# Causal attention: the order of VectorE's work inside one turn

## The reference, cut to what matters

```
k = (x @ Wk).reshape(B, H, T, hs)
q = (x @ Wq).reshape(B, H, T, hs)
v = (x @ Wv).reshape(B, H, T, hs)
wei = jnp.einsum('bhtd,bhsd->bhts', q, k) * scale
mask = jnp.tril(jnp.ones((T, T), dtype=bool))
wei = jnp.where(mask, wei, -jnp.inf)
wei = jax.nn.softmax(wei, axis=-1)
out = jnp.einsum('bhts,bhsd->bhtd', wei, v).reshape(B, T, C)
return out @ Wp + bp                        # added to the tokens
```

## Time and profile before

| | |
|---|---|
| median of 3 runs | 1110.09 us (1109.1 to 1111.11) |
| the profiled execution | 1110.88 us, with a span of 1109.1 us |
| TensorE busy in the span | 1006.5 us, 91% |
| VectorE, ScalarE, GpSimd busy | 61%, 55%, 53% |
| mean granted TensorE clock | 0.971 |

### The profile page before, as it was taken

The page is one execution under the profiler, slowest core; times in us unless marked ns, Lnnn a source line. Parts: engine busy times, 40 slices in busy tenths (PEclk is TensorE's granted clock), DMA queues, the critical chain, the costliest instruction groups (busy, mean ns, idle before and its releaser), DMA issues. The chain is left out here.

```text
span 1109.1 us, 29005 instructions
## 1 busy us (share of the span) xinstructions
PE 1006.5 (91%) x11022; PEld 681.8 (61%) x11022; DVE 676.6 (61%) x1880; ACT 610.5 (55%) x1662; POOL 593.2 (53%) x788
## 2 busy tenths in 40 slices
PE   5999989799979799999999997787988988999998
PEld 2677755467745476767676765455665565566665
DVE  2899944499956355656566663576776686433332
ACT  1666633367733366666666663545665564456553
POOL 4667538477665355454545446344465545373632
PEclk9999999899989999999999998889999999999999
DMA  6500000000000000000000000000000000000000
GB/s 126 97 6 2 2 1 3 1 1 3 1 2 2 1 1 1 2 1 2 1 1 1 2 2 1 2 1 2 1 1 2 2 1 2 2 16 9 16 9 16
DMA packets 28248, 9.65 MB, mean 9 GB/s; under 512 B 26513, under 2 KB 28112, under 8 KB 28112
## 3 DMA queue, kind: packets, MB, share of 16 engines
q1 hardware_dynamic: 25088, 6.89, 3.0%
q10 hardware_dynamic: 3024, 0.92, 0.4%
HBM read 6.23 MB, written 1.57 MB: 7 GB/s over the span
## 5 line engine op out<-in xcount | busy, mean ns | idle before, releaser
L1140 POOL TENSOR_TENSOR fa_e<-fa_e,fa_rc 128x1024 f32<-128x1024 f32 x64 | 120.5, 1893 | 142.3 <-DVE fa_rc L1363 142.3
L1653 POOL TENSOR_TENSOR ca_e<-ca_e,ca_rc 128x256 f32<-128x256 f32 x96 | 76.7, 826 | 84.0 <-DVE ca_rc L1978 84.0
L1297 ACT ACTIVATE fa_e<-bank,fa_nm 128x256 f32<-128x256 f32 x256 | 118.6, 497 | 0.0
L1884 ACT ACTIVATE ca_e<-bank,ca_nm 128x128 f32<-128x128 f32 x192 | 78.0, 430 | 51.0 <-DVE ca_nm L1964 51.0
L2183 ACT ACTIVATE ex_G<-bank,e_b 128x512 f32<-128x512 f32 x96 | 64.4, 687 | 50.2 <-PE bank L137 47.5
L137 PE MATMUL bank<-hT,e_w 96*64 96x512 f32 x384 | 88.6, 596 | 0.0
L2255 DVE SCALAR_TENSOR_TENSOR X<-bank,ex_L,X 128x96 f32<-128x96 f32 x128 | 31.7, 310 | 88.9 <-PE bank L137 82.4
L1357 DVE TENSOR_REDUCE fa_nm<-bank 128x4 f32<-128x1024 f32 x64 | 75.5, 1219 | 14.6 <-PE bank L1166 14.6
L137 PEld LDWEIGHTS bank<-e_w,ex_G 128*64 128x64 f32 x1536 | 67.2, 137 | 17.2 <-issue 10.5
L167 POOL TENSOR_TENSOR ln_r<-ln_v,minus_half 128x2 f32<-128x2 f32 (+2 forms) x85 | 75.7, 890 | 0.0
L186 DVE TENSOR_TENSOR X<-X,bank 128x192 f32<-128x192 f32 (+1 forms) x72 | 30.0, 418 | 71.8 <-PE bank L137 54.2
(11 more groups left out here) (247 smaller groups left out, 2395.1 us busy)
## 6 DMA issues: line engine op xcount, KB each, us to landing
out_tokens<-X SPq DMA_DIRECT2D x8, 192.0 KB, 2.1
X<-in_x SPq DMA_DIRECT2D x14, 96.0 KB, 3.2
e_w<-in_L_ffn_w SPq DMA_DIRECT2D x2, 576.0 KB
bias0r<-in_L_conv_rpb_table ACTq DMA_DIRECT2D x16, 24.0 KB
m0w<-in_L_conv_mlp_w SPq DMA_DIRECT2D x2, 144.0 KB
m1w<-in_L_conv_w SPq DMA_DIRECT2D x2, 144.0 KB
f_w<-in_L_ffn_W SPq DMA_DIRECT2D x2, 142.5 KB
mixer<-in_mixer SPq DMA_DIRECT2D x1, 256.0 KB
```

The lines of the kernel that those rows point to most:

```text
L1140: pool.tensor_tensor(e, e, r.broadcast_to([P, 4, TOK]), ALU.mult).then_inc(s["nrm"], 1)
L1297: last = act.activation(E[v % 4][:, i, c, :], bank[b + i][:, c * TOK:(c + 1) * TOK], ACT.Exp, bias=NM[v % 4][:, i, c:c + 1], accum_out=SU[ ...
L1653: last = pool.tensor_tensor(e, e, RC[u % 2][:, images, c, :].broadcast_to([P, 2, (c + 1) * P]), ALU.mult)
L1884: last = act.activation(E[u % 2][:, j, keys(c)], bank[j][:, keys(c)], ACT.Exp, bias=NM[u % 2][:, j, c:c + 1], accum_out=SU[u % 2][:, j, c: ...
```

## The change

Only the order of VectorE's functions in a turn changes. Before, both pairs' maxima stand first, then the three copies, inverse 0, the slot's own work and inverse 1. After, it is maxima 0, copy 0, maxima 1, copy 1, inverse 0, copy 2, statistics (in the slots that have them), inverse 1, and then the projection's copy or the residual. No instruction is added or removed, and no wait changes. The `yield` of turn 0, at which the block before goes on, keeps its place.

```diff
             if c < STEPS:
                 maxima(c, 0)
-                if c == 0:
-                    yield
+            if c == 0:
+                yield
+            if 1 <= c <= STEPS:
+                turned_out(c - 1, 0)
+            if c < STEPS:
                 maxima(c, 1)
             if 1 <= c <= STEPS:
-                for f in range(FILLS):
-                    turned_out(c - 1, f)
+                turned_out(c - 1, 1)
             if c < STEPS:
                 inverse(c, 0)
+            if 1 <= c <= STEPS:
+                turned_out(c - 1, 2)
+            if h in (0, 4) and n >= 2 and c < STEPS:
+                statistics(dve, k, s, 2 * (n - 2) + h // 4, 4)
+            if c < STEPS:
+                inverse(c, 1)
             if h in (1, 2, 3) and fetch:
                 project(m, 2 * (h - 1) + 1, 6)
             elif h == 5 and n >= 1:
                 for half in range(2):
                     residual(n - 1, half)
-            elif h in (0, 4) and n >= 2 and c < STEPS:
-                statistics(dve, k, s, 2 * (n - 2) + h // 4, 4)
-            if c < STEPS:
-                inverse(c, 1)
```

## The result

The changed kernel takes 1114.53 us as the median of 20 executions, against 1109.91 for the kernel before in 20. The ratio is 1.0034, with a 95% interval of 1.0021 to 1.0047. It is slower by about 0.3%, where I had forecast a gain of 1.4 us, and the time lies above my range of 1106.6 to 1111.0. Two of the 20 executions of the changed kernel took 1106.41 and 1106.62, where the other 18 took 1112.0 to 1117.7; the kernel before has such executions too (1106.67 and 1107.10), so they say little about the order.

A forecast was written before the change was run, and what follows sets the result against it. The prediction took TensorE's causal attention stretch, 177 of 1109.1 us, as bounding, with waits for copies. Terms 1.12 + 0.44 + 0.12 + 0.59 - 0.50 - 0.30 - 0.1 = 1.37 gave median 1108.7 us, range 1106.6 to 1111.0.

The forecast's parts named there:

- rival on the clock: Low stretches at turn 19 and before turn 7 go, about 0.5 us each: 1107.4 us, chance 0.22.
- The projecting turns: Slots 1 to 3: projection 1 starts earlier, gated by copy 1; 0.28 us gained in turns 7, 8, 13, 14, total 1.12.
- turn 2: Projecting turn with 1.12 us of waiting for GpSimd; the earlier inverse was to gain 0.44 us.
- turn 3: Slot 3, values transposed ahead of the turning: copy 0 waits, so only 0.12 us gained.
- Turns 9 and 15: Output projection next waits for heads_out; inverse 1 ahead of the projection's copy ends it no earlier, so nothing was counted.
- Slot 5: Turns 11 and 17: copy 2 starts 0.25 us later and delays the second output transpose; 0.50 us lost in all.
- Turn 19: TensorE at half clock: copy 0 waits and holds the second maxima, ScalarE starts late; 0.30 us lost.
- The end: Turn 23: inverse 0 releases GpSimd earlier and scaling goes on without a gap; last values 0.59 us earlier.
- late maxima: Copy 0 holds maxima 1 in 11 turns bound by ScalarE, 0.30 us each: slower, 1111.7 us, chance 0.10.
- the cover of 0.05: ScalarE-bound turns: second maxima ready at M+3.03, needed by M+3.08, when copy 0 doesn't wait.
- The moved gate: VectorE's row gets tighter; each added change of instruction kind costs 0.07 us, the 0.28 go: 1109.8 us, chance 0.18.
- the likeliest case: The forecast itself, 1.4 us of gain: spans 1108.0 to 1109.6 us by its small terms' bounds, chance 0.50.

The follow-up runs named there:

- fillers_after_23: Changed kernel with four extra matmuls, no part of the computation, in each turn of slots 4, 5 and the last group, none after turn 23: 1107.46 us.
- fillers_after: Changed kernel with four extra matmuls, no part of the computation, in each turn of slots 4 and 5 and the last group, also after turn 23: 1108.61 us.
- best_with_fillers: Kernel before with new order in slots 0 to 3 of first three groups and from turn 23; two extra matmuls per non-projecting turn up to 23: 1106.43 us.
- copies_only: Kernel before with only the copies moved between the maxima as in the changed kernel, inverses left where they were: 1111.80 us.
- best_order_bare: Kernel before with new order only in slots 0 to 3 of the first three groups and from turn 23 on, no extra matmuls: 1111.40 us.

## Why the prediction was wrong, point by point

**The failed step is the clock.** The sum treated the low stretches as a fixed background: turn 1 and turn 19 were priced at half clock, all others at full. The one rival on the clock asked only whether the two known falls would go, and the argument was that turns 4, 5 and 18 are not made denser. I didn't ask the reverse, whether the same work in another order would bring more falls. It brought 17 us more of low clock (23.9 against 6.8), and the loss from it, 5.7 us, is more than the whole gain of the order. The prediction's list of signs names low clock in other places as one of being wrong, but none of its rivals and chances stand for it. The turns show the price (M to the next M; for turn 23 to the experts' first matmul):

| turn | before | changed | changed order at full clock |
|---|---|---|---|
| 3 | 6.44 | 6.33 | 6.33 |
| 4, 5 | 5.99, 6.16 | 6.36, 7.07 | 6.01, 6.00 |
| 6 | 7.39 | 7.39 | 6.67 |
| 7 | 6.43 | 7.75 | 6.17 |
| 13, 14 | 6.43, 6.43 | 6.17, 6.17 | 6.17, 6.17 |
| 11, 17 | 6.38, 6.38 | 6.61, 6.61 | 6.60, 6.61 |
| 12 | 6.81 | 6.66 | 6.68 |
| 19, 20 | 6.19, 5.72 | 6.53, 6.22 | 6.18, 5.74 |
| 22 | 5.72 | 5.85 | 5.86 |
| 23 | 10.87 | 12.15 | 10.28 |

The last column is fillers_after_23 in its turns at full clock (its two falls hit turns 7 and 13, which are taken from fillers_after and best_with_fillers). The changed kernel lies above it by 0.35 + 1.07 + 0.72 + 1.58 + 0.35 + 0.48 + 1.87 = 6.4 us in turns 4, 5, 6, 7, 19, 20 and 23. The kernel before paid 0.16 + 0.58 = 0.7 for its own low stretches, in turns 5 and 6. The difference, 5.7, less the order's gain of 1.6 (below) is 4.1, and the spans differ by 4.0. That the clock is the step that failed is shown by this and by the fillers; why the new order brings more falls stays open.

**The projecting turns** were right: 0.26 in each of turns 7 (at full clock), 8, 13 and 14 where I had 0.28, gated by copy 1; 0.43 in turn 2 (6.59 to 6.16) where I had 0.44; 0.11 in turn 3 where I had 0.12. Turns 9 and 15 lost 0.07 and 0.11 to the later heads_out, where I had put nothing. The text's own figures give 0.46 for turn 2 (6.59 less 6.13); it wrote 0.44.

**Slot 5** was right: 0.23 lost in turns 11 and 17, forecast 0.25. TensorE's timeline of the changed kernel in turn 11 answers to the earlier trace rows, and its longer wait is in it:

```profile
850.38 1.54 PE L1730 MATMUL bank<-ident,ca_e 128*128 128x128 f32 x12
853.29 1.21 PE L1804 MATMUL bank<-ident,ca_oc 96*128 96x96 f32 x8 [1.37 <-DVE ca_et L1971]
```

**Turn 19** was right in its step and wrong in where the fall stands. In the changed kernel turn 19 was at full clock until 911.39, near its end, so the loss of 0.30 had no occasion there. But copies_only has the copies between the maxima, and its fall lies in turn 19 as in the kernel before. Rows of TensorE, VectorE and ScalarE there:

```profile
903.97 0.61 PE L1695 MATMUL bank<-causal,identb 128*128 128x256 bf16 x4
...
905.07 2.77 PE L1730 MATMUL bank<-ident,ca_e 128*128 128x128 f32 x12
...
906.17 0.69 DVE L1971 COPY ca_et<-bank 128x512 f32<-128x512 f32 x1 [0.74 <-PE bank L1730]
906.78 1.01 DVE L1964 TENSOR_REDUCE ca_nm<-bank 128x2 f32<-128x256 f32 x2
...
907.83 0.37 ACT L1884 ACTIVATE ca_e<-bank,ca_nm 128x128 f32<-128x128 f32 x1 [0.17 <-DVE ca_nm L1964]
```

Copy 0 waits 0.74, and ScalarE starts the second pair at M+3.86, where it was M+3.57 (907.35 less 903.78). The turn lasts 6.48 instead of 6.19: 0.29 lost, forecast 0.30. What the rival on the clock priced too high is the fall's own cost: turn 19 lasts 6.18 at full clock with either order, so in the old order the low stretch cost nothing, and not 0.5.

**The end** was right in mechanism and size (0.59, in best_order_bare and fillers_after_23), and hidden in the changed kernel by two falls.

**The rivals.** At full clock late maxima came out at 0.14 in turn 22 and at nearly nothing in the others, so the cover of 0.05 was enough but for that turn. (The prediction counts eleven turns bound by ScalarE where its words, slot 4 and all from 18, name nine; with nine its time is 1111.1 in place of 1111.7.) The moved gate did not come: changes between kinds of instruction cost nothing in turn 14 (0.94, 0.60, 0.93, 0.59 from start to start). The first of the two rules, from the Trainium skill, Perfetto Trace Analysis, section Tensor Engine Instruction, is that VectorE is strict FIFO. It held in the rows shown: maxima 1 stayed behind the waiting copy 0 in copies_only. The second rule, that an idle stretch throttles TensorE and activity frees it, is of the Trainium skill, TensorE: Matmul & The Clock Gate, section Part 1. The fillers agree with it in the main: with four in each light turn the profiled executions had one fall and two, where there were six. The traces don't bear it out whole. The longest wait in the 10 us ahead of any fall of the changed kernel is 1.27 us (for the values of turn 4), and the fall left in fillers_after came with TensorE busy for 9.93 of 10.00 us.

At equal clock the order is worth 1.6 us: from the start of turn 2 to the experts it is 157.0 us in fillers_after_23 with the low stretches taken out (0.69 in each of turns 7 and 13), against 158.7 before. The sum without its 0.30 for turn 19 is 1.7. That the two agree so closely is in part luck, as terms that the sum had small or at nothing differ in sign: turn 6 gained 0.14 and turn 12 0.13, turns 9, 15 and 22 lost 0.32 together. The span of the likeliest case was also a little too wide for its bounds: 0.6 lost to 0.5 gained give 1108.1 to 1109.2.

## What to carry to other kernels

Ahead of any change of order, list the stretches where TensorE waits often and look up whether its clock falls in or near them. If a trace has even one low stretch in such a place, give the clock a rival on the slower side, and test with filler matmuls in the waits: they show what the order is worth by itself. A reordering that makes other engines early can take away short waits that broke up a long one; here that is an explanation that fits the two orders, and it is not shown. Compare single turns at the same granted clock, as the median of a whole kernel mixes the two effects.

## What the runs showed of the hardware

The falls came behind stretches that were far from idle. In the changed kernel TensorE was busy for 8.0 of the 10.0 us ahead of one (805.75 to 815.75), in waits of 0.9 us and less; ahead of the fall in turn 4 the longest wait was 1.3 us. In fillers_after it was 9.93 of 10.00.

The output projection of turn 21 ran at 0.50 from 925.0 to 928.5 in the changed kernel, and lost nothing: from 923.99 to the next M it is 5.50, against 5.51 at full clock in the kernel before (from 921.37). There the fall had no price, while in turn 7 it cost 1.58. Over all turns one microsecond of low clock cost 0.27 us here (6.4 over 23.9). That other engines set the pace of light turns would explain why it isn't more; turn 19 in the old order, as long at 0.50 as at full clock, fits that.
